# Two-hop graph layer: units of late columns taken through both hops in columns 2 and 3, and column 0's marks reordered

## What is computed

```python
h  = maximum(layernorm(x), 0)
x1 = swish((adj @ h)  @ W0 + b0)          # first hop
x2 = swish((adj @ x1) @ W0 + b0)          # second hop
x  = x + x2
h  = maximum(layernorm(x), 0)
a_hat = adj + eye
d     = sum(a_hat, axis=1) ** -0.5
x  = x + ((a_hat * d[:, None] * d[None, :]) @ h) @ W1.T + b1   # third product
```

## Time and profile before

| | us |
|---|---|
| median of 3 runs (1441.64 to 1442.49) | 1441.7 |
| the profiled execution, its own time | 1441.8 |
| its span, first to last instruction | 1438.7 |
| PE busy | 1385.1 (96%) |
| DVE busy | 1008.3 (70%) |
| ACT busy | 684.1 (48%) |
| POOL busy | 36.6 (3%) |

### The profile page before, as it was taken

One profiled execution on the slowest core, in us unless ns is written; L12 is line 12 of the kernel. 1 busy time (PEld: TensorE's weight loads), 2 busy tenths in 40 slices (PEclk: granted clock), 3 DMA queues, 4 the chain that ended last, 5 costly groups with the idle time before them and its releaser, 6 DMA issues.

```text
span 1438.7 us, 18318 instructions
## 1 busy us (share of the span) xinstructions
PE 1385.1 (96%) x6598; PEld 650.1 (45%) x6598; DVE 1008.3 (70%) x2334; ACT 684.1 (48%) x781; POOL 36.6 (3%) x30
## 2 busy tenths in 40 slices
PE   3788999999999999999999999999999999999998
PEld 1333444444444444444444544454444444444444
DVE  7978889999877876875774777876665555546331
ACT  7788888887767757647650122222311321132000
POOL 1100000000000000000000010101000000000000
PEclk9999999999999999999999999999999999999999
DMA  9999999999999888887750111112433334332000
GB/s 378 366 419 421 418 415 421 422 415 400 377 365 383 336 323 338 337 325 294 304 236 30 38 59 60 67 67 68 159 148 123 116 127 153 118 130 112 23 15 24
DMA packets 56255, 335.49 MB, mean 233 GB/s; under 512 B 6240, under 2 KB 6752, under 8 KB 18272
## 3 DMA queue, kind: packets, MB, share of 16 engines
q1 hardware_dynamic: 49104, 322.20, 56.4%
q10 hardware_dynamic: 7056, 12.06, 2.3%
HBM read 322.44 MB, written 11.80 MB: 232 GB/s over the span
## 4 chain that ended last, share of the span: by engine, by line
PE 86%; DMA 8%; DVE 3%; issue 2%; ACT 2%; POOL 0%; SPq 0%; DVEq 0%; ACTq 0%
PE acc_ps L589 21%; PE acc_ps L588 21%; PE acc_ps L530 12%; PE acc_ps L529 12%; DMA ring<-adj 8%; PE early_ps L499 6%; PE early_ps L498 6%; PE z_ps L481 3%; PE kept_ps L507 2%; PE kept_ps L508 2%; ACT marks L664 1%; DVE ring L345 0%; PE kept_ps L589 0%; PE kept_ps L588 0%; DVE marks L850 0%
## 5 line engine op out<-in xcount | busy, mean ns | idle before, releaser
L709 ACT ACTIVATE unused<-ring 128x2048 uint8<-128x2048 uint32 x220 | 419.9, 1909 | 79.5 <-DMA ring<-adj 67.9
L529 PE MATMUL acc_ps<-marks,node_a 128*128 128x512 fp8e4 x1024 | 393.4, 384 | 45.8 <-DVE node_a L843 29.6
L530 PE MATMUL acc_ps<-marks,node_a 128*128 128x512 fp8e4 x1024 | 393.5, 384 | 1.5 <-issue 1.5
L589 PE MATMUL acc_ps<-ring,node_a 128*128 128x512 fp8e4 x1024 | 388.8, 380 | 0.0
L588 PE MATMUL acc_ps<-ring,node_a 128*128 128x512 fp8e4 x1024 | 388.5, 379 | 0.0
L850 DVE TENSOR_SCALAR marks<-ring 128x2048 uint8<-128x2048 f32 x226 | 277.6, 1228 | 69.5 <-DMA ring<-adj 45.8
L345 DVE TENSOR_SCALAR ring<-bits 128x256 uint32<-128x256 uint32 (+1 forms) x784 | 159.6, 280 | 89.4 <-PE acc_ps L589 89.3
L529 PEld LDWEIGHTS acc_ps<-marks,node_a 128*128 128x128 f16 x1024 | 101.0, 99 | 180.2 <-issue 65.7
L750 ACT ACTIVATE nT<-acc_ps 128x512 f32<-128x512 f32 x16 | 9.6, 597 | 313.3 <-PE acc_ps L589 313.3
L499 PE MATMUL early_ps<-marks,node_b 128*128 128x512 fp8e5 x416 | 158.0, 380 | 0.0
L589 PE MATMUL acc_ps<-ring,node_b 128*128 128x512 fp8e5 x416 | 157.9, 380 | 0.0
(11 more groups left out here) (117 smaller groups left out, 1110.0 us busy)
## 6 DMA issues: line engine op xcount, KB each, us to landing
ring<-adj SPq DMA_DIRECT2D x256, 1024.0 KB, 7.8
marks<-adj SPq DMA_DIRECT2D x36, 1024.0 KB, 5.0
node_b<-x SPq DMA_DIRECT2D x4, 1024.0 KB, 13.1
xch<-x SPq DMA_DIRECT2D x16, 256.0 KB, 2.8
xn_scratch<-xnew ACTq DMA_DIRECT2D x16, 256.0 KB, 2.0
xch<-xn_scratch SPq DMA_DIRECT2D x16, 256.0 KB, 2.9
out<-xnew ACTq DMA_DIRECT2D x16, 256.0 KB, 2.0
part_scratch<-stage ACTq DMA_DIRECT2D x13, 256.0 KB, 5.0
```

Of the source, the lines that this page charges most:

```text
L529: nc.tensor.matmul(acc_ps[c % 2][:, :], hi_of(node_a16, j), byte, start=(j == 0), stop=False)
L530: last = nc.tensor.matmul(acc_ps[c % 2][:, :], lo_of(node_a16, j), byte, start=False, stop=(j == NB - 1))
L589: last = nc.tensor.matmul(into[:, :], lo_of(node, j), byte.bitcast(low), start=False, stop=closes)
L709: nc.scalar.activation(unused[:, :], slot(g).bitcast(U32), ACT.Sign, accum_out=nz_count[:, g:g + 1]).then_inc(counted, 1)
```

## The change

1. **Units ahead.** Four places are put into the order, after tiles 7 and 11 of column 2 and after tiles 7 and 11 of column 3. At each, the tiles 0 and 1 of two later columns (13 and 14, 11 and 12, 9 and 10, 7 and 8) are loaded, marked by DVE, multiplied for the first hop (16 matmuls a column, into the accumulator that the column under way doesn't use) and then for the second (16 matmuls, into `early_ps`). ACT saves the two sums: `save_x` into a part of `bits` that is not written yet, `save_y` into a part of `node_b`. In columns 7 to 14 the tiles 0 and 1 are then left out (`hole`), and POOL adds the saved sums to `stage` and to nT. No matmul is added or dropped.
2. **Column 1's finish comes earlier.** The second hop ahead needs the features of columns 0 and 1, so in column 2 the steps from `sums_out` to `low_part` are some tiles earlier (`FINISH_FIRST`).
3. **Late tiles.** The 16 tiles ahead are counted in the third phase: `LATE` has 52 tiles, four to a step. The matmul that sums the flags is one step later.
4. **Column 0.** DVE marks tile 10 ahead of the pack and of `h_low` of tile 8, `h_low(3)` comes before `first_rest(3)`, the feature scales start one tile later, and ACT's `make_h` parts 3 to 7 are one or two tiles later.
5. **Small loads.** The second layer's weight and bias are loaded by SP after all tiles, no longer by ACT at the start.

```diff
-LATE = list(range(TC)) + ACT_MARKED[10:]
-LATE_STEP = 3
-H_BEFORE = {1: (0, 1), 2: (2,), 5: (3,), 6: (4,), 8: (5,), 10: (6,), 12: (7,)}
+AHEAD = {2 * TC + 7: (13, 14), 2 * TC + 11: (11, 12), 3 * TC + 7: (9, 10), 3 * TC + 11: (7, 8)}
+AHEAD_COLUMNS = [c for pair in AHEAD.values() for c in pair]
+LATE = list(range(TC)) + ACT_MARKED[10:] + [c * TC + i for c in sorted(AHEAD_COLUMNS) for i in range(2)]
+LATE_STEP = 4
+H_BEFORE = {1: (0, 1), 2: (2,), 6: (3,), 8: (4,), 10: (5,), 12: (6,), 14: (7,)}
...
+FINISH = {"sums out": 2, "project": 4, "bias": 7, "scale": 8, "sigmoid": 8, "gate": 10, "high": 11, "low": 14}
+FINISH_FIRST = {"sums out": 1, "project": 3, "bias": 5, "scale": 6, "sigmoid": 5, "gate": 7, "high": 7, "low": None}
...
+            for c in sorted(AHEAD_COLUMNS):
+                pair = AHEAD_COLUMNS.index(c)
+                pool.wait_ge(early_ready, c - KEPT + 1)
+                pool.wait_ge(y_saved, pair + 1)
+                nc.gpsimd.tensor_tensor(halves(stage), halves(stage), saved_y(c), ALU.add).then_inc(stage_added, 1)
+                pool.wait_ge(sums_part, c - FIRST_AHEAD + 1)
+                pool.wait_ge(x_saved, pair + 1)
+                nc.gpsimd.tensor_tensor(half(nT, c % 2), half(nT, c % 2), saved_x(c), ALU.add).then_inc(nT_ready, 1)
...
+            def unit_ahead(now, pair, c, at):
+
+                into = acc_ps[(now + 1) % 2]
+                pe.wait_ge(nT_ready, now)
+                if pair > 0:
+                    pe.wait_ge(x_saved, pair)
+                for i in range(2):
+                    pe.wait_ge(marked, marked_upto(at + i))
...
+                last.then_inc(x_done, 1)
+                if pair > 0:
+                    pe.wait_ge(y_saved, pair)
+                if now >= KEPT:
+                    pe.wait_ge(early_ready, now - KEPT + 1)
...
+            def save_x(c):
+                act.wait_ge(x_done, AHEAD_COLUMNS.index(c) + 1)
+                nc.scalar.mul(saved_x(c), acc_ps[(AHEAD_IN[c] + 1) % 2][:, :], 1 / (ONE * H_SCALE)).then_inc(x_saved, 1)
+
+            def save_y(c):
+                act.wait_ge(tile_mm, multiplied_upto(AHEAD_AT[c] + 1))
...
+                    if e.ahead:
+                        first, second = AHEAD[OWN_BEFORE[e.at]]
+                        if (c, i) == (second, 1):
+                            save_x(first)
+                            save_y(first)
+                        continue
...
+                    if g - 1 in AHEAD:
+                        save_x(AHEAD[g - 1][1])
+                    if g - 2 in AHEAD:
+                        save_y(AHEAD[g - 2][1])
...
                     if g == 6:
                         first_stats(3)
-                        mark(8)
+                        mark(ORDER[8])
+                        h_low(3)
                         first_rest(3)
+                        mark(ORDER[10])
```

More of the change, by code:

```diff
@@ new lines, with __init__, entries @@
+class Entry:
+    def __init__(self, at, g, ahead=False):
+        self.at, self.g, self.ahead = at, g, ahead
+        self.c, self.i = g // TC, g % TC
+        self.hole = not ahead and self.c in AHEAD_COLUMNS and self.i < 2
+def entries():
+    order = []
+    for g in range(NC * TC):
+        order.append(Entry(len(order), g))
+        for c in AHEAD.get(g, ()):
+            for i in range(2):
+                order.append(Entry(len(order), c * TC + i, True))
+    return order
+ORDER = entries()
@@ new lines, with units_of, groups_upto, marked_upto @@
+LOADED = [e for e in ORDER if not e.hole]
+LOAD_AT = {e.g: a for a, e in enumerate(LOADED)}
+OWN = {e.g: e.at for e in ORDER if not e.ahead}
+GROUPS = len(ORDER) // 4
+def units_of(r):
+    return range(1 if ORDER[4 * r].hole else 0, 2)
+def groups_upto(c):
+    return OWN[c * TC + TC - 1] // 4 + 1
+def marked_upto(at):
+    return sum(e.g not in ACT_MARKED and not e.hole for e in ORDER[:at + 1])
+def act_marked_upto(at):
+    return sum(e.g in ACT_MARKED and not e.hole for e in ORDER[:at + 1])
@@ new lines, in signed_upto, with multiplied_upto @@
+def signed_upto(at):
+    return sum(e.g not in LATE and not e.hole for e in ORDER[:at + 1])
+def multiplied_upto(at):
+    return sum(not e.hole for e in ORDER[:at + 1])
+SIGNED = signed_upto(len(ORDER) - 1)
+OWN_BEFORE = {e.at: max(h for h in AHEAD if OWN[h] < e.at) for e in ORDER if e.ahead}
+AHEAD_AT = {e.c: e.at for e in ORDER if e.ahead and e.i == 0}
+AHEAD_IN = {c: g // TC for g, pair in AHEAD.items() for c in pair}
+SAVED_BY = {now + 1: 2 * sum(g < (now + 1) * TC for g in AHEAD) for now in sorted({g // TC for g in AHEAD})}
@@ L374, in _ @@
                 load_tile(part)
[L375 to L378, removed]
[L379 to L383 removed]
+            for a, e in enumerate(LOADED[RING:]):
+                had = LOADED[a]
+                if had.g in ACT_MARKED:
+                    sp.wait_ge(act_marked, act_marked_upto(had.at))
+                else:
+                    sp.wait_ge(marked, marked_upto(had.at))
+                if had.g not in LATE:
+                    sp.wait_ge(counted, signed_upto(had.at))
+                load_tile(e.g)
+            sp.dma_start(w_sb[:, D:2 * D], w1t).then_inc(w1_in, 16)
+            sp.dma_start(b_sb[:, D:2 * D], b1.to_broadcast([P, D])).then_inc(w1_in, 16)
             sp.wait_ge(tile_mm, NC * TC)
[L387 removed]
+            sp.wait_ge(bits_ready, GROUPS)
             for k, n in enumerate(SECOND_ORDER):
@@ new lines, in _ @@
+            for e in ORDER:
+                    c, i, g = e.c, e.i, e.g
+                    if e.ahead:
+                        if i == 0:
+                            unit_ahead(ORDER[e.at - 1 - AHEAD_COLUMNS.index(c) % 2 * 2].c, AHEAD_COLUMNS.index(c), c, e.at)
+                        continue
+                    if i == 0:
+                        kept = [(n, q) for q in range(CB) for n in range(2 if c == 2 else KEPT)] if c >= 2 else []
+                        kept_at = KEPT_AFTER[:len(kept)]
+                        done = 0
+                    if e.hole:
+                        continue
+                    opens = 2 if c in AHEAD_COLUMNS else 0
@@ L998, in _ @@
                 first_rest(part)
-            for c in range(NC):
-                for i in range(TC):
-                    g = c * TC + i
-                    r = g // GT
-                    if g not in ACT_MARKED and g != 8:
-                        mark(g)
-                    if c == 0 and i % 2 == 0:
+            for e in ORDER:
+                    c, i, g = e.c, e.i, e.g
+                    r, place = e.at // GT, e.at % GT
+                    if g not in ACT_MARKED and g not in (8, 10) and not e.hole:
+                        mark(e)
+                    if c == 0 and i % 2 == 0 and i != 6:
                         h_low(i // 2)
```

217 lines of the change are left out of this document (132 added, 85 removed).

## The result

| | before | after |
|---|---|---|
| median, us (6 runs each, beside each other) | 1441.64 (1440.64 to 1442.49) | 1433.64 (1431.27 to 1436.16) |
| ratio, 95% interval | | 0.9949 [0.9939, 0.9959] |
| the profiled execution, its own time | 1441.8 | 1431.94 |
| its span | 1438.7 | 1430.1 |
| from the start of the last projection to the end of the span | 6.3 | 8.4 |

The change makes the kernel 8.0 us faster by the medians, 5.9 to 8.8 by the interval of the ratio; forecast 7.0.

A forecast was written before the change was run, and what follows sets the result against it. Loads bound PE up to column 3, PE's own work after it. 1441.8 less 6.0 (10.9 lost behind 116.4 us, 4.9 staying) less 1.0 for column 0 is 1434.8, 1434.7 for the median; range 1428.5 to 1440.5.

The forecast's parts named there:

- the prediction's own sign: Prediction wrong if waits without releaser sum to over 8 or under 3 us, PE waits for marks, or a step grows.
- PE becomes the bound in columns 2 and 3: Columns 2 and 3: with units ahead, PE's work exceeds the loads, 61.4 against 59.8 us in column 2.
- The distances: Projection of column 1 to column 2, 296 matmuls, 64.9 us; to column 3, 304 matmuls, 66.6 us; waits without releaser extra.
- the saved sums that POOL adds: POOL's 16 additions, 1.49 us each on an idle engine: costed at nothing; without cover 12 us.
- The waits for tiles go, 3.3 us: PE's waits for tiles, all in column 3: 3.3 us, called the sure gain.
- The two waits without releaser stay: PE's waits of 3.2 and 1.7 us (at 121.06 and 203.83 us), expected again in about the same places: 4.9 us stay.
- The Trainium skill's rule that a crossing is mostly hidden: Rival "No wait for instructions": nothing of the 4.9 us stays behind 116.4 us, giving 1429.8; chance 0.20.
- The clock doesn't fall again: PE's granted clock, 0.50 after the first wait without releaser, costing 2.7 us: taken as not recurring, kept as an end.
- Column 0, 1.0 us: Column 0, 35 to 65 us: a tile freed earlier regains load time; bounds nothing and 3.7 us, 1.0 taken.
- ACT held by PE: Slower rival: saves at the four places delay ACT's counts; a chain 6 us longer costs 3.1 each, 1447.2; chance 0.08.
- The cover of 2.8 us a place: At each place ahead, PE's 14.7 us of work against ACT's chain of 11.9 us leaves 2.8 us of cover.
- The late tiles cost nothing: Third phase, 16 more tiles: DVE gets 2.3 us more a step, under 4.4 spare; steps stay 28.5 us.

The follow-up runs named there:

- the run without an instruction wait: Changed kernel with 40 unused one-column matmuls in column 1's tiles 8 to 15, shifting later PE code: 1432.29 us, ratio 0.9941.
- experiment 3: 28 unused matmuls (6.0 us) in front of tile 9 of column 2: in the kernel before 1441.45 us, in the changed kernel 1439.41 us.
- the three kernels with shifted PE code: Changed kernel with 40 tiny unused matmuls in column 1: alone 1432.29 us, with 40 unused ACT operations 1429.97, with 120 1432.78.
- experiment 4: 40 unused one-column matmuls in column 1's tiles 8 to 15: in the changed kernel 1432.29 us, in the kernel before 1440.57 us.
- experiment 6: Changed kernel with ACT counting the first tile behind each of the four places four times instead of once: 1446.57 us, ratio 1.0039.
- the repetition: The changed kernel run again, unedited, for a second profile: 1433.81 us, ratio 0.9946.
- experiment 2: Parts of the change: column 0 and small loads without units ahead 1438.88 us; units ahead with old column 0 order 1434.42; places only in column 2 1436.81.
- experiment 5: Changed kernel with 40 tiny PE matmuls, plus unused ACT operations in the third phase: 40 give 1429.97 us, 120 give 1432.78 us.

## Why the prediction was right

The time (1434.7 forecast, 1433.64 measured) and the cause hold, but one term failed by the prediction's own sign, and the terms' errors partly cancel. By its steps:

- **PE becomes the bound in columns 2 and 3.** Right, with the loads close behind it: in the earlier trace rows DMA stands at 9 for thirteen slices, not for ten as the prediction read it, so the loads keep their engines full well past column 5. The distances were forecast as 64.9 and 66.6 us without waits; measured 66.3 and 67.1 with 1.3 and 0.4 of waits, and 65.3 in the run without an instruction wait. An added stop of 6.0 us costs 5.6 to 5.8 there, and at most 2.6 in the kernel before (experiment 3). The matmuls are the same 6598; in columns 7 to 14 each distance is 6.9 us shorter, the forecast 32 matmuls (the first 35.5 instead of 42.4, the last 47.6 instead of 54.5). So the saved sums that POOL adds in these columns cost nothing, as forecast.
- **The waits for tiles go, 3.3 us.** Right but for 0.4 in the change's profile. The parts apart show it: with places in column 2 only, 3.1 us of waits for marks are there again. That PE never waits for a tile from tile 5 of column 2 on is too strong: where the stop is gone, such waits come back further on (0.8 to 1.7 us behind 115 us in the three kernels with shifted PE code).
- **The two waits without releaser stay, 4.9 us.** This is the term that was mis-sized. One stayed, 1.4 us instead of 3.2; the other is gone. The prediction had set 3 us as the least of their sum; at 1.4 it is wrong by that sign. 8.7 us were gained behind 116.4 instead of 6.0. That these waits are tied to places in the code was shown (experiment 4). That they are paid in full once PE is the bound was not: an added stop is, but the profiles without this one are no shorter up to column 5. So the ledger's attribution of 1.4 us to it, and the prediction's rule for both, overstate what their removal gives. Why the one shrank isn't settled. By its row it has 1.3 us in the profiles of the change and with the units ahead alone, 2.8 with column 0 alone. The Trainium skill's rule that a crossing is mostly hidden (Runtime: NRT & Kernel Launch, Instruction fetch mechanics) agrees with the trace in part: one stop of 1.4 us is left in this stretch of the changed kernel, and none in the kernels with shifted code.
- **The clock doesn't fall again.** Right: 1.00 in both stretches. It fell to 0.66 behind three of the four waits of 2.2 to 4.3 us in experiment 6.
- **Column 0, 1.0 us.** Too small in most profiles: 2.0 in the profiled execution of the change, 1.8 (2.2 by medians) alone, but 0.7 in the repetition. The rate from 35 to 65 us rose from 369 to 378 only, which makes 9 x 30 / 421 = 0.6 us; the rest came outside that stretch. Most of it is the order, not the small loads (experiment 2).
- **ACT held by PE.** It happens as the rival describes it, ACT's waits from 112 to 250 us:

```profile
ACT bits L798 <- PE acc_ps L613: 32.8, 8, 8.1
ACT node_b L803 <- PE early_ps L626: 14.8, 8, 2.9
```

  47.6 us in sum, while all of PE's waits for marks in this stretch are 0.4. The cover of 2.8 us a place was right to 0.4 on average (experiment 6); with a margin as thin as this the rival was a real one.
- **The late tiles cost nothing.** Right. A step is 28.5 us as before; DVE is busy 18.50 in it instead of 15.84 and still has waits of 4.17 and 1.92 for tiles:

```profile
1029.03 2.29 DVE L1294 TENSOR_SCALAR_CACHE_REDUCE count_a<-marks 128x2048 uint8<-128x2048 f32 x1 [4.17 <-DMA marks<-adj]
...
1033.24 2.29 DVE L1294 TENSOR_SCALAR_CACHE_REDUCE count_a<-marks 128x2048 uint8<-128x2048 f32 x1 [1.92 <-DMA marks<-adj]
```

- **The ending was left out of the sum**, as if nothing in it could move. It cost 2.1 us in the profiled execution (2.6 in the repetition). So two gains were bigger than forecast, 2.7 behind 116.4 and 1.0 at the front, and 2.1 were lost at the end: 1.6 more in sum than the 7.0 forecast, by the profile.

So the near hit of the number is in part luck, errors of opposite sign, while the mechanism stands on experiments 2, 3 and 6.

## What to carry to other kernels

A stop of an engine that isn't the bound is worth little to remove, and a stop added to the engine that is the bound costs its full length. The two are not mirror images: removing a stop from the new bound pays only until the next bound is met, here the loads two columns later. So price each stall again under the new bound, in both directions, before adding it up. Work that is moved into idle time paid in the columns where it was put, and the queue that carries its results (here ACT's saves) has to be costed with its slack: of 6.3 us more in it at each place 3.2 were covered, and the rest turned the gain of 8.0 us into a loss. Once a kernel is tuned to a few us, the mere number of instructions can be worth as much as a change of order (2.5 us at the end here); a few dozen idle instructions are a cheap trial.

## What the runs showed of the hardware that wasn't expected

- **Instruction waits have a fixed place.** Both waits of the kernel before (121.06 and 203.83 us) recur at the same matmuls in the run with column 0 alone (2.8 and 1.8 us), and the first in both profiles of the change; with shifted code both are gone. In PE's records (weight loads, matmuls and semaphore instructions) the two are 768 instructions apart, three times 256. A third, in the run with places in column 2 alone, is 1024 records behind the first, four times 256:

```profile
222.65 0.24 PE L576 MATMUL misc_ps<-ones,count 128*128 128x1 f16 x4 [1.08 <-issue]
```

  The Trainium skill (Runtime: NRT & Kernel Launch, Instruction fetch mechanics) has 256 instructions in a block of 16 KB; the distances agree, and one instruction packet moves in the 3.3 us up to the wait of the change. The borders between them show no wait, and why these three do isn't known.
- **The last jump.** The Trainium skill (Runtime: NRT & Kernel Launch, Instruction fetch mechanics) says that a taken branch whose target isn't in the window of loaded pages forces a fetch before execution goes on. The runs fit this: 3.1 us against under 0.5, switched on and off by the number of ACT's instructions (experiment 5). That the fetch itself is what takes the time was not measured, and the packets don't tell the two endings apart. DMA queues from 1426.5 to 1430 us (packets, MB, share), first in the changed kernel with its long ending, then in the kernel with 40 ACT operations more and the short one:

```profile
q8 instruction: 1, 0.02, 1.7%
q14 instruction: 2, 0.02, 1.6%
```

```profile
q14 instruction: 2, 0.02, 1.9%
q8 instruction: 1, 0.02, 1.8%
```

- **Some small DVE operations take over five times as long beside POOL.** In column 0 of the change:

```profile
40.58 1.04 POOL L525 TENSOR_SCALAR node_a<-node_b 128x1024 f16<-128x1024 f32 x1 [3.93 <-ACT node_b L814]
```

```profile
40.50 0.19 DVE L233 TENSOR_TENSOR tmp<-stats 128x16 f32<-128x16 f32 x1
40.72 0.93 DVE L234 SCALAR_TENSOR_TENSOR tmp<-tmp 128x16 f32<-128x16 f32 x1
41.68 0.18 DVE L235 SCALAR_TENSOR_TENSOR var<-mv,tmp 128x16 f32<-128x16 f32 x1
```

  The operation that starts under POOL's ends with it; the same line takes 0.16 to 0.18 us the nineteen other times it runs. Two more of this size do the same in the same profile (L233 at 16.35 us, 1.01; L226 at 19.49, 0.94), while batch-norm statistics under a POOL operation take 0.27 to 0.28 us one after the other. No run tested it.
